# A fifth pair of seven products in each row of a two-layer expert kernel, and its token sums made in the first phase

## What is computed

```
def gemma_mlp(x, g, u, d):            # 256 -> 1024 -> 256
    return (gelu_tanh(x @ g) * (x @ u)) @ d
w, sel = top_k(softmax(cond_8), 2);  w = w / w.sum()
x = x + sum_e dense_w[:, e] * gemma_mlp(x, skill_gate[e], skill_up[e], skill_down[e]) \
      + gemma_mlp(x, shared_gate, shared_up, shared_down)
x = x + x @ W_base.T + b_base + 2 * lora(x, As, Bs, cond_8)
```

## Time and profile before

| | |
|---|---|
| median of 3 runs | 801.58 us (801.01 to 801.67) |
| profiled execution, its time | 802.68 us |
| its span, first to last instruction | 800.9 us |
| PE busy, matmuls | 792.9 us, 4140 |
| PEld busy | 683.3 us |
| DVE busy | 673.1 us |
| ACT busy | 478.2 us |
| POOL busy | 282.7 us |
| granted PE clock | 0.999 of full speed |

### The profile page before, as it was taken

How to read it: one execution, slowest core, us unless ns; L and a number is a source line. 1 busy time by engine, 2 the same in 40 slices (tenths; PEclk the granted TensorE clock), 3 DMA queues, 4 the chain that set the end, 5 groups by cost and what they waited for, 6 DMA issues and landing times.

```text
span 800.9 us, 13422 instructions
## 1 busy us (share of the span) xinstructions
PE 792.9 (99%) x4140; PEld 683.3 (85%) x4140; DVE 673.1 (84%) x910; ACT 478.2 (60%) x737; POOL 282.7 (35%) x284
## 2 busy tenths in 40 slices
PE   9999999999999999999999999999999999999998
PEld 8888888887888888888988888988888888898887
DVE  3886887886976899988988898898888889889886
ACT  5564564564554656666666675666666566566663
POOL 1530321421110683253352345325345333533520
PEclk9999999999999999999999999999999999999999
DMA  6346526307413333373454265336246525631400
GB/s 198 86 120 194 148 80 194 122 1 250 132 40 80 118 121 117 134 196 106 139 197 126 81 207 160 118 132 194 88 128 218 135 79 191 173 104 57 131 2 27
DMA packets 138191, 102.59 MB, mean 128 GB/s; under 512 B 62865, under 2 KB 131217, under 8 KB 138129
## 3 DMA queue, kind: packets, MB, share of 16 engines
q1 hardware_dynamic: 138128, 101.91, 42.3%
HBM read 78.29 MB, written 23.59 MB: 127 GB/s over the span
## 4 chain that ended last, share of the span: by engine, by line
PE 91%; DVE 5%; DMA 2%; issue 1%; SPq 0%; ACT 0%; POOL 0%; DVEq 0%; POOLq 0%; ACTq 0%
PE ps_ring L808 56%; PE ps_acc L808 33%; DMA xbuf<-xt_scratch 2%; DVE xc L1493 1%; DVE inner_lo L1493 1%; DVE wide L1493 1%; DVE post L1829 1%; PE ps_ring L928 1%; PE ps_acc L1017 0%; PE ps_acc L922 0%; DVE post L1752 0%; PE ps_acc L1037 0%; DVE post L1559 0%; SPq L500 0%; DVE post L1761 0%
## 5 line engine op out<-in xcount | busy, mean ns | idle before, releaser
L808 PE MATMUL ps_ring<-xc,wide 128*128 128x512 f32 (+1 forms) x1938 | 419.2, 364 | 2.3 <-DVE post L1761 1.4
L808 PEld LDWEIGHTS ps_ring<-xc,wide 128*128 128x128 f32 x1938 | 338.9, 189 | 63.2 <-DVE post L1761 2.0
L1144 ACT CAST inner_hi<-post 128x512 fp32r<-128x512 f32 x192 | 117.7, 620 | 105.2 <-DVE post L1829 34.9
L808 PE MATMUL ps_acc<-inner_hi,wide 128*128 128x512 f32 x504 | 171.0, 390 | 0.0
L1493 DVE TENSOR_TENSOR inner_lo<-post,inner_hi 128x512 fp32r<-128x512 f32 x192 | 146.9, 772 | 8.7 <-ACT inner_hi L1144 5.8
L1147 ACT ACTIVATE post<-ps_ring 128x512 f32<-128x512 f32 (+1 forms) x125 | 67.9, 545 | 98.4 <-PE ps_ring L808 94.5
L808 PEld LDWEIGHTS ps_acc<-inner_hi,wide 128*128 128x128 f32 x504 | 94.7, 188 | 19.1
L808 PE MATMUL ps_acc<-inner_lo,wide 128*128 128x512 f32 x252 | 98.4, 391 | 0.0
L1147 ACT ACTIVATE post<-post 128x256 f32<-128x256 f32 (+1 forms) x98 | 53.7, 563 | 57.2 <-DVE post L1770 39.4
L808 PE MATMUL ps_acc<-inner_hi,sh_dn 128*128 128x512 f32 x256 | 83.8, 389 | 0.0
L690 POOL TENSOR_TENSOR post<-post 128x512 f32<-128x512 f32 x24 | 31.0, 1293 | 137.6 <-DVE post L1548 137.6
(11 more groups left out here) (128 smaller groups left out, 1016.4 us busy)
## 6 DMA issues: line engine op xcount, KB each, us to landing
rights_scratch<-xc SPq DMA_DIRECT2D x6, 1792.0 KB, 9.5
raw<-n_L_cond_skill_gate_dram SPq DMA_DIRECT2D x32, 256.0 KB, 3.0
raw<-in_L_cond_skill_up_dram SPq DMA_DIRECT2D x32, 256.0 KB, 3.5
raw<-n_L_cond_skill_down_dram SPq DMA_DIRECT2D x32, 256.0 KB, 3.9
xbuf<-n_L_cond_skill_gate_dram SPq DMA_DIRECT2D x32, 256.0 KB, 2.9
xbuf<-in_L_cond_skill_up_dram SPq DMA_DIRECT2D x32, 256.0 KB, 3.4
xbuf<-n_L_cond_skill_down_dram SPq DMA_DIRECT2D x32, 256.0 KB, 3.7
xt_scratch<-xbuf SPq DMA_DIRECT2D x8, 512.0 KB, 3.2
```

Source lines behind the costliest of these rows:

```text
L808: last = pe.matmul(dst, left_[a], right_[b], start=start and n == 0, stop=stop and n == len(PASSES) - 1, skip_group_check=adds)
L1144: return nc.scalar.copy(dst, src)
```

## The change

1. `SEVEN` has five pairs, 1, 2, 4, 5 and 7 (before 1, 3, 5, 7); row 0 does pairs 4, 5 and 7. So 38 pairs of the second phase are of seven products instead of 31. Pairs 1 and 2 follow each other directly, and so do 4 and 5.
2. The block A21 of a seven pair is not split any more: its split is of 1280 elements (`but_a21`). The weights lie otherwise in `raw` and `wide` so that the rest is two equal pieces.
3. A row's splits are reordered, as are layer 1's parts: `layer1_lo` and the split of the effective weights at step 4, `layer1` and `turn_output` at 6, the fold of the low-rank part at 12 and 13. Pair 3's weights are split in two parts, at steps 1 and 2. POOL's `row_sum` stands behind pair 4's `ex_c22`.
4. The token sums of rows 0 and 1 are made in the first phase, on POOL in units 13 and 14. Those of row 1 are stored, and loaded again in row 0. Row 0's tokens are loaded ahead of the last `store_rights`, not behind it.
5. At the start: 13 dummy transposes and 5 more behind the first real ones, instead of 20; the first gate weights come in two DMAs; unit 0 is reordered. The routing moves from units 2 and 3 to 7, 11 and 15, the exponential to unit 14.

```
-    SEVEN = [1, 3, 5, 7]
-    FIRST_SEVEN = SEVEN[1:]
+    SEVEN = [1, 2, 4, 5, 7]
+    FIRST_SEVEN = SEVEN[2:]
...
-        SPLIT_FIRST = {0: 2, 2: 3, 5: 4, 6: 5, 9: 6, 10: 7, 13: 8, 14: 9}
-        SPLIT_LATER = {1: 2, 4: 3, 6: 5, 9: 6, 10: 7, 13: 8, 14: 9}
-        SUMS_FIRST = {4: 1, 8: 2, 12: 3}
-        SUMS_LATER = {0: 0, 8: 2, 12: 3}
+        SPLIT_FIRST = {0: 2, 2: 3, 5: 4, 7: 5, 8: 6, 10: 7, 12: 8, 14: 9}
+        SPLIT_LATER = {0: 2, 6: 4, 7: 5, 8: 6, 10: 7, 12: 8, 14: 9}
+        SUMS_FIRST = {4: 2, 7: 3, 10: 4, 13: 5}
+        SUMS_LATER = {0: 1, 4: 2, 10: 4, 13: 5}
...
+                if seven:
+                    take_lo(but_a21(ex_all(1, j)), but_a21(raw[j]), but_a21(ex_all(0, j))).then_inc(weights_ready, 1)
+                else:
+                    take_lo(ex_all(1, j), raw[j], ex_all(0, j)).then_inc(weights_ready, 1)
...
@@ POOL, first phase
+                if u == NU - 3:
+
+                    pool.wait_ge(sh_stored, 32 * (Q - 1))
+                    sums_of_x(0)
+                if u == NU - 2:
+                    pool.wait_ge(ex_t_ready, 1)
+                    sums_of_x(1)
...
@@ PE, a seven behind a seven waits for DVE's reads of the banks
+                    if n < 3 and k // 2 - 1 in sevens_of(first):
+                        pe.wait_ge([ex_mul, ex_c_done, ex_c_done][n], [3 * st - 2, 2 * st - 1, 2 * st][n])
...
@@ DVE, a row
+                            if k == X1_LO_STEP and not first:
+                                layer1_lo(b - 1)
+                                fold_lo(b - 1)
+                            if k in sums_at:
+                                split_sums(sums_at[k])
...
@@ PE, start
-            for _ in range(20):
+            for _ in range(13):
                 pe.transpose(ring[3][:, 0:P], ident[:], ident[:])
...
+            for _ in range(5):
+                pe.transpose(ring[3][:, 0:P], ident[:], ident[:])
```

More of the change, by code:

```diff
@@ L50, in cond_resid_kernel @@
     assert PAIRS == 4 and Q == 4
[L52 removed]
+    L1_STEP = 6
     CONST_STEP = 3
@@ L269, in cond_resid_kernel @@
         ex_c12 = inner[1]
-        gate0_landed = sem("gate0_landed")
+        gate0_landed = [sem(f"gate0_landed{c}") for c in range(HC)]
         up0_landed = sem("up0_landed")
@@ L418, in seventh @@
         def seventh(b, k, first):
-            return sum(2 * pr < k for pr in sevens_of(first)) + (0 if first else b * NS - 1)
+            return sum(2 * pr < k for pr in sevens_of(first)) + (0 if first else b * NS - WHOLE_FIRST)
         def whole(b, k, first):
             now = k - 2 * sum(2 * pr < k for pr in sevens_of(first))
-            return now if first else b * (K - 2 * NS) + 2 + now
+            return now if first else b * (K - 2 * NS) + 2 * WHOLE_FIRST + now
         def seven_no(b, n_s):
-            return b * NS + n_s - 1
+            return b * NS + n_s - WHOLE_FIRST
         block = ctx.enter_context(nc.Block())
@@ L523, in _ @@
             store_xt(0, 0)
+            sp.wait_ge(turned, 4)
+            load_x_blocks(3, x_blk1)
             store_xt(0, 1)
@@ L968, in seven_products @@
                     elif n == 3:
-                        pe.wait_ge(gelu_done, whole(b, k, first))
+                        pass
                     elif n in (4, 5):
@@ L975, in seven_products @@
                         last = product(ring[bank][:, part * HS:(part + 1) * HS],
-                                       [ex_left(n_s, hl, part, a_) for hl in range(2)],
+                                       [ex_left(par, n_s, hl, part, a_) for hl in range(2)],
                                        [ex_right(par, hl, b_) for hl in range(2)],
@@ L1329, in _ @@
                     split_routed_gu(0, 0, jr, product_done, products(u, UP, NP - 1))
+                if u == NU - 3:
+                    split_sums_x([sums_x(0, n) for n in range(2)], 0)
                 if j == 0:
@@ L1793, in split_pair, with split_sums @@
                         split_routed(b + 1, 0, pr - 2 * PAIRS, pr - 2 * PAIRS in SEVEN)
+                def split_sums(n_s):
+                    if n_s < NS:
+                        split_sums_w(b, par, n_s)
+                    elif not last:
+                        split_sums_w(b + 1, 1 - par, n_s - NS)
                 def fold_sum():
```

382 lines of the change are left out of this document (211 added, 171 removed).

## The result

| | before | now |
|---|---|---|
| median | 800.8 us (6 runs, 799.85 to 801.67) | 808.82 us (6 runs, 808.47 to 809.75) |
| ratio | | 1.0102 [1.0089, 1.0115] |
| span of the profiled execution | 800.9 us | 807.9 us |
| PE busy | 792.9 us | 793.9 us |
| DVE busy | 673.1 us | 701.5 us |

The account below looks back on a forecast made before the run. PE was taken to bound the later rows, DVE most of row 0. Terms -2.65 - 1.0 - 2.6 - 0.4 + 0.7 = -5.95 us from 802.68 gave 796.7, or 795.6 as median; range 793.0 to 800.6.

Parts of the forecast that it names:

- the one on the later rows: Rows 1 to 7: a fifth seven pair makes PE wait for DVE, 0.1 us a row, +0.7 us in all.
- Products: Second phase, PE: 7 more pairs of seven products save 0.38 us each, -2.65 us.
- Row 0's tokens: First phase, unit 12: loading them ahead of the stores removes the wait and the slow restart, -1.0 us.
- Row 0's stalls: Row 0: less work on DVE and POOL recovers 2.6 of 2.9 us of PE stalls; bounds 0 and -2.9.
- Start: Kernel start: two fewer dummy transposes ahead of the first product, -0.4 us; bounds 0 and -1.4.
- What was costed at nothing ahead of row 0: Units 13 to 15: token sums ready in time, exponential's table load covered by idle time; 0 us, table load up to +2.6.
- Pairs 4 and 5: Between these neighbouring sevens: DVE has 2.9 us for other work, needs 1.8 to 3.4; stall 0 to 0.5 a row.
- Only the worst of all three passes the slack: Pair 5: split of pair 6, `row_sum` slowing DVE's splits and pair 4's late start; hence only 0.1 us a row taken.
- The sums of busy time: Later rows: DVE busy about 62.0 of 66.84 us, POOL 30.5; on the sum of its work DVE still fits.
- the 64 us: Sign of being wrong: DVE busy for over 64 us of one row of the loop.
- B: Rival: pair 5's three burdens coincide, one 0.97 us stall in each of 7 rows, 6.8 us, 801.7 us; chance 0.12.
- C: Rival, steps 6 to 12: DVE and POOL take turns, 1.6 us a row, 11.4 in all, 806.3 us; chance 0.09.

Follow-up runs that it names:

- the small weight sums: The changed kernel with POOL's four sums of each pair's weights in the second phase cut from 128 to 8 columns of each block: 796.21 us, ratio 0.9939.
- the fastest kernel: The changed kernel with `row_sum` on DVE instead of POOL and the loops of ACT and DVE written out: 796.52 us, ratio 0.9947.
- The part alone: The kernel before with row 0's tokens and pair 2's weights loaded ahead of the last two 1792 KB stores: 800.52 us, ratio 1.0002.
- Four sevens with the token sums moved: The kernel before with the changed start, token sums in the first phase and row 0's tokens loaded ahead of the stores: 797.03 us, ratio 0.9951.

## Why the prediction was wrong

The step that failed is the one on the later rows, +0.7 with the bounds 0 and +3.5. It was +14.1 us of waits against 2.7 of gain.

- **Products, -2.65.** The pieces cost what was said. The shortest rows take 66.97 to 67.04 us instead of 66.84, and the traces show the difference as one short wait for DVE's first addition, at pair 5 with the small weight sums (0.13 us) and at pair 4 in the fastest kernel: there the addition ends at 421.81, the last product starts at 421.86, and pair 5 starts 7.95 us behind pair 4 instead of 7.78. So the term was right; what no kernel reached is a row without any such wait.
- **Row 0's tokens, -1.0.** The wait is gone from the trace, but its size was that of one execution. The part alone gave 1.0002 [0.9993, 1.0012], a second trace had a wait of 0.27 us instead of 0.94.
- **Row 0's stalls, -2.6.** Row 0 went from 79.52 to 76.83, 2.7 (2.2 beside the second trace of the kernel before, where it lasts 79.06). Four sevens with the token sums moved give 76.44, so it is the token sums and not the order of the splits.
- **Start, -0.4.** PE's first product came at 6.97 us instead of 7.67, 0.7.
- **What was costed at nothing ahead of row 0** held: the token sums ended at 214.07 and 227.30 us (214.9 and 228 were forecast), and PEld's only wait there is 0.48 us, for DVE.
- **Pairs 4 and 5, +0.7.** The sum had the right form. Pair 4's first addition was to be 2.2 us behind PE's start of the pair, with up to 0.7 more. It was 3.6 behind (419.87 to 423.48), so 1.4 late. This is the size that was wrong: ahead of step 7's multiplication DVE idled for 0.96 us, until ACT had split the second set of weight sums, and ACT had waited for POOL's fourth sum:

```profile
417.93 1.05 ACT L1198 CAST xc<-stage 128x1024 fp32r<-128x1024 f32 x1 [1.25 <-POOL stage L802]
```

With the small weight sums the addition came 2.45 us behind PE's start (417.22 to 419.67). The way from there to pair 5's addition was to be 6.3 + 1.8, with up to 0.9 for `row_sum`: 9.0. It took 8.91, and that this fits is luck: it takes 7.36 without `row_sum`, and `row_sum` adds 1.55. I had counted only the two splits as slowed (0.92), not the two multiplications ahead of them (2.18 us instead of 0.48 + 0.75). With the slack of 1.4 the formula gives 1.4 + 8.91 - 7.78 - 1.4 = 1.13 us a row. PE lost 1.13, though the last digit agrees by chance: pair 5 started 7.90 us behind pair 4 and not 7.78, and 0.10 of the loss is the slow restart. "Only the worst of all three passes the slack" was the mistake beside that size: the worst of all three is what a loop repeats in each row, since none of them is a matter of chance.
- **The loop's branch** stood in no case. It cost 1.8 and 1.7 us at rows 3 and 5. Before, ACT idled for 2.10 us and DVE for 1.07 at the same place, and the profile put that down to PE and to ACT. The timelines of ACT and DVE in the kernel before, at the start of row 3:

```profile
457.83 0.60 ACT L1147 ACTIVATE post<-ps_ring 128x512 f32<-128x512 f32 x1 [2.10 <-PE ps_ring L808]
```
```profile
459.19 0.75 DVE L1829 SCALAR_TENSOR_TENSOR post<-post,coef_now,ps_ring 128x512 f32<-128x512 f32 x1 [1.07 <-ACT post L1147]
```

That was right for the greater part: at the start of row 2, where no branch stands, ACT idles for 1.40 us and DVE for 0.51. The branches added only the other 0.7 and 0.56, and PE waited for neither. With four sevens and ACT's loop written out the time stays the same (797.14 against 797.03), and DVE still idles for 1.07 us at the start of row 3 and 0.50 at that of row 2, so that its share is from its own branch.
- **The sums of busy time.** DVE was forecast at 62.0 us a row and POOL at 30.5; in the changed kernel they have 64.2 and 33.4 in the mean of rows 1 to 6, and two of the stretches above pass the 64 us that the prediction named as a sign of being wrong (64.39 and 66.21). The fastest kernel has DVE at 62.27 with hardly a wait, so the sum of the work was right, and what the engines cost each other came on top.

Of the rivals, B had the mechanism: one wait at pair 5 of every row. Its 6.8 us for seven rows were 7.9; with the branches (3.5) and the small waits (2.7) added, 801.7 + 1.1 + 3.5 + 2.7 comes to 809.0, where 808.8 was measured. C had the sign and the cause of most of it, POOL slowing DVE, at 806.3. C was held less likely because the row of before had shown no stall at a like sum; that row also had no pair of neighbours. The rule that stood beside C, in the Trainium skill, "SBUF — State Buffer", section "SBUF: two separate sides", says which operations of DVE are hit: among others those with two SBUF inputs. The traces agree with that: beside POOL the splits go from 0.69 to 1.2 us, while the additions that read PSUM keep their 0.68. Whether a split is blocked for the whole of a POOL operation, as the rule has it, these rows don't decide: one that waited for all of a POOL operation (0.74 us and more) would lose more than the 0.5 us seen, one that came in its middle would not.

## What to carry to other kernels

Where two pieces of work follow each other at a fixed distance, lay out the engine's whole queue between them with the durations that its operations have beside the others' work, and take the worst case as the normal one: a loop repeats it. An operation on POOL can cost more of DVE's time than DVE would need to do it itself (here 1.6 against 1.2 us). And put a loop's branch, on each engine, where that engine has 3 us to spare, or write the loop out: what hid it before may be gone after a change that has nothing to do with it.

## What was not expected of the hardware

- In the changed kernel and in the one with ACT written out, a branch back costs ACT 2.60 us and DVE 2.8 us until the next instruction is given out, in loops of two rows. What was queued ahead still runs. The Trainium skill, "Advanced Engine Details and Errata", section "Control Flow Timing", gives a compare-and-branch about 108 ns; here the branch itself took 0.04 to 0.06 us, and the time until the next instruction is some 25 times that figure. POOL's branch (L845, a loop of one row), by contrast, was followed by 0.22 us in the chain of the changed kernel. What the engines do in that time was not tried.
- The wait for one DMA (row 0's tokens in unit 12) left PE waiting for 0.94 us in one execution and 0.27 in another. A profile is one execution, and a term that rests on one DMA's landing should have a second.
